# One pool of seven PSUM banks, with each stage taking the bank expected free first, in a fused attention and feed-forward kernel

## The reference

```python
x  = hidden_states                      # (8, 512, 128), fp32
x  = x + layernorm(attn(layernorm(x)))  # 16 heads: A = tril(taylor_exp(q) @ taylor_exp(k).T), y = A @ v, RMS norm, @ Wo
x  = x + layernorm(ffn(layernorm(x)))

def ffn(x):                             # six layers
    for i in range(6):
        x = attn_layer(shift_tokens(x), ...) + x   # local attention, window 32, 16 heads of 64
        x = ffn_layer(shift_tokens(x), ...) + x    # layernorm, W1, a * gelu(gate), W2
    return x

def attn_layer(x, Wqkv, qs, ks, Wo):
    q, k, v = split(x @ Wqkv)
    q, k = rotary(l2norm(q) * qs), rotary(l2norm(k) * ks)
    return local_attention(q, k, v) @ Wo           # softmax of 32 queries over their own and the previous 32 keys
```

## Time and profile before

| | |
|---|---|
| median of 3 runs | 3474.63 us (3473.0 to 3476.83) |
| the profiled execution | 3475.88 us, span of its profile 3474.1 us |
| busy: TensorE, VectorE, ScalarE, GpSimd | 92%, 80%, 73%, 59% |
| granted TensorE clock, mean | 0.979 |
| 700 to 3400 us: TensorE busy | 2506.3 of 2700 us |
| 700 to 3400 us: VectorE busy | 2296.6 us |
| 40 to 560 us: TensorE busy | 495.8 of 520 us |

### The profile page before, as it was taken

The page is one execution under the profiler, slowest core; times in us unless marked ns, Lnnn a source line. Parts: engine busy times, 40 slices in busy tenths (PEclk is TensorE's granted clock), DMA queues, the critical chain, the costliest instruction groups (busy, mean ns, idle before and its releaser), DMA issues.

```text
span 3474.1 us, 125058 instructions
## 1 busy us (share of the span) xinstructions
PE 3179.2 (92%) x52744; PEld 1975.5 (57%) x52744; DVE 2763.6 (80%) x3420; ACT 2536.5 (73%) x5866; POOL 2044.8 (59%) x1559
## 2 busy tenths in 40 slices
PE   7999997899999999999999899999999999999986
PEld 3444434566666566656666566666666665655553
DVE  3656657888888888888888888888888888888883
ACT  4666664778777777768787878787777777787784
POOL 0000006767677666767677777677767676766661
PEclk9999998999999999999999999999999999999998
DMA  3223324444444444444444444444444444434431
GB/s 110 77 75 80 80 57 135 140 142 136 145 149 145 135 134 145 144 140 137 140 136 148 138 151 138 140 141 152 146 142 137 134 146 139 143 127 145 137 130 31
DMA packets 271821, 447.01 MB, mean 129 GB/s; under 512 B 84254, under 2 KB 122396, under 8 KB 271132
## 3 DMA queue, kind: packets, MB, share of 16 engines
q1 hardware_dynamic: 244944, 422.50, 37.3%
q10 hardware_dynamic: 26316, 16.52, 1.7%
HBM read 124.21 MB, written 7.34 MB: 38 GB/s over the span
## 4 chain that ended last, share of the span: by engine, by line
PE 47%; DVE 24%; ACT 13%; issue 7%; SPq 3%; DMA 2%; POOL 2%; DVEq 0%; ACTq 0%; POOLq 0%
PE PS L542 47%; DVE TPB L938 8%; ACT SC L1245 8%; DVE SM L973 2%; DVE MX L962 2%; ACT SX L1221 2%; DMA RB<-root_scratch 2%; DVE NV L953 2%; DVE NV L951 1%; DVE PP L981 1%; POOL K L1332 1%; DVE H L1006 1%; SPq L477 1%; DVE NV L955 1%; ACT H L1024 1%
## 5 line engine op out<-in xcount | busy, mean ns | idle before, releaser
L938 DVE SCALAR_TENSOR_TENSOR TPB<-PS,VEC,C 128x1024 f32<-128x1024 f32 x768 | 959.1, 1269 | 98.7 <-ACT SX L1221 91.2
L1245 ACT ACTIVATE SC<-PS,BQ,RQ 128x64 f32<-128x64 f32 x3072 | 977.7, 437 | 40.0 <-DVE BQ L967 39.8
L1221 ACT ACTIVATE SX<-PS 128x512 f32<-128x512 f32 x768 | 468.6, 638 | 355.0 <-PE PS L542 347.9
L1332 POOL TENSOR_TENSOR K<-K,RB 128x512 f32<-128x512 f32 x384 | 496.2, 1292 | 286.8 <-DMA RB<-root_scratch 273.4
L1358 POOL TENSOR_TENSOR SC<-SC,RC 128x1024 f32<-128x1024 f32 x192 | 366.1, 1907 | 409.3 <-DVE RC L975 409.3
L542 PE MATMUL PS<-LXH,LH 128*128 128x512 f32 x768 | 379.2, 494 | 153.3 <-DVE TPB L938 145.9
L1350 POOL TENSOR_TENSOR K<-TPB,TR 128x512 f32<-128x512 f32 x384 | 499.2, 1300 | 0.0
L1350 POOL TENSOR_TENSOR Q<-TPB,TR 128x512 f32<-128x512 f32 x384 | 497.6, 1296 | 0.0
L542 PEld LDWEIGHTS PS<-PP,VV 64*64 64x64 f32 x12288 | 279.8, 136 | 149.7 <-issue 146.2
L542 PE MATMUL PS<-PP,VV 64*64 64x96 f32 (+1 forms) x12288 | 352.6, 250 | 4.3 <-DMA PP<-PX 2.0
L542 PE MATMUL PS<-AOT,LO 128*128 128x512 f32 x768 | 342.4, 599 | 0.0
(11 more groups left out here) (166 smaller groups left out, 5862.8 us busy)
## 6 DMA issues: line engine op xcount, KB each, us to landing
TR<-TPB SPq DMA_DIRECT2D x768, 256.0 KB, 2.7
RB<-root_scratch SPq DMA_DIRECT2D x768, 128.0 KB, 3.0
PP<-PX SPq DMA_DIRECT2D x576, 64.0 KB
PP<-PP SPq DMA_DIRECT2D x384, 64.0 KB, 2.4
WS<-in_wqkv ACTq DMA_DIRECT2D x72, 128.0 KB, 2.5
PP<-PX SPq DMA_DIRECT2D x192, 48.0 KB
QA<-TH SPq DMA_DIRECT2D x128, 64.0 KB, 2.1
QA<-TL SPq DMA_DIRECT2D x128, 64.0 KB, 2.1
```

Of the source, the lines that this page charges most:

```text
L938: e.scalar_tensor_tensor(TPB[:, n % 3:4 + n % 2:3 + n % 2 - n % 3, w, :], g, VEC[:, l, 9 + w:10 + w], C[:, at:at + 1024].rearrange("p (o c ...
L1221: e.activation(SX[i % 3][:, :], bk("PJ", key)[:, :], ACT.Square).then_inc(sem["pj_act"], 1)
L1245: p = e.activation(SC[m % 2][:, g, :, :].rearrange("p x k -> p (x k)"), bank[s][:, at:at + 64], ACT.Exp, bias=BQ[m % 2][:, g:g + 1], scale ...
L1332: e.tensor_tensor(dst, dst, RB[n % 2][:, :], ALU.mult).then_inc(sem["pr_pool"], 1)
```

## The change

All seven banks but bank 4 form one ring. Each claim says until when the planner expects the bank to be held (`held`, the difference of two places), and `take` gives the bank whose `until` is smallest. S1 and PV claim two banks each with `pair`, and each reads its banks through `bk`. Since the two banks need not be neighbours, MX becomes two reductions and PVn two copies. SX gets a fourth buffer. `PLACE` isn't changed.

```diff
-        self.ring, self.busy = [], {}
+        self.ring, self.busy, self.until, self.now = [], {}, {}, 0
...
-                at = self.ring.pop(0)
-                self.ring.append(at)
+                at = self.take(self.ring, 1, self.now)[0]
...
+    def take(self, ring, n, until):
+        banks = sorted(ring, key=lambda at: self.until.get(at, 0))[0:n]
+        for at in banks:
+            ring.remove(at)
+            ring.append(at)
+            self.until[at] = until
+        return banks
...
         for t, i, f, a, kw in sorted(plan, key=lambda e: e[:2]):
+            o.now = t
             f(*a, **kw)
...
+        if kind == "end":
+            o.until[o.bank["N2", (kind, b), 0]] += SLOT * (P["EN"][2] - P["EN"][1])
...
     def switch():
-        o.first = [o.busy[i] for i in early]
-        o.ring = [5, 6, 7]
+        o.ring = [0, 5, 6, 7] + early
+        o.busy[0] = ("as_act", 24 * NB)
         o.busy[5] = ("ao_act", NB)
...
-    def group(st, i, by, value):
-        ring = early or o.ring
-        at = ring.pop(0)
-        ring.append(at)
+    def group(st, i, by, value, held=0):
+        at = o.take(early or o.ring, 1, o.now + SLOT * max(held, 0))[0]
...
+    def pair(st, key, by, value, held):
+        for i, at in enumerate(o.take(o.ring, 2, o.now + SLOT * max(held, 0))):
+            o.hold(at, st, key, i)
+            o.busy[at] = (by, value)
+        o.put(st, *key)
...
-            lay(z + j + P["VP"], group, "VP", 8 * u + j, "vp_act", 8 * u + j + 1)
+            lay(z + j + P["VP"], group, "VP", 8 * u + j, "vp_act", 8 * u + j + 1, P["VC"] - P["VP"])
...
-            lay(n + P["PJ"][w], group, "PJ", i, "pj_dve", i + 1)
+            lay(n + P["PJ"][w], group, "PJ", i, "pj_dve", i + 1, P["PT"][w] - P["PJ"][w])
...
+            lay(n + P["S1"], pair, "S1", (m,), "s3_act", 4 * m + 4, max(P["S3"]) - P["S1"])
...
+            lay(n + P["PV"][0], pair, "PV", (m, 0), "pv_act", m + 1, P["PVn"] - P["PV"][0])
...
-        SX = [sb(f"SX{i}", [128, L]) for i in range(3)]
+        SX = [sb(f"SX{i}", [128, L]) for i in range(4)]
...
-                    if m:
-                        on.wait_ge("s3_act", 4 * m)
+                    for s in range(2):
+                        free(on, st, key, s)
...
-                        if p:
-                            on.wait_ge("pv_act", p)
+                        for x in range(2):
+                            free(on, st, key, x)
...
-                    e.tensor_reduce(MX[:, :], g, AX_X, ALU.max).then_inc(sem["s1_dve"], 1)
+                    for s in range(2):
+                        g = bk("S1", key, s).rearrange("p (g k) -> p g k", k=64)
+                        p = e.tensor_reduce(MX[:, 8 * s:8 * s + 8], g, AX_X, ALU.max)
+                    p.then_inc(sem["s1_dve"], 1)
...
-                    if i > 2:
-                        on.wait_ge("ss_pe", i - 2)
+                    if i > 3:
+                        on.wait_ge("ss_pe", i - 3)
...
-                    e.copy(AOT[:, 2 * p % 8:2 * p % 8 + 2, :], PS[:, 2:4, :]).then_inc(sem["pv_act"], 1)
+                    for x in range(2):
+                        y = e.copy(AOT[:, 2 * p % 8 + x, :], bk("PV", (p, 0), x))
+                    y.then_inc(sem["pv_act"], 1)
```

More of the change, by code:

```diff
@@ L256, in order @@
         for j in range(8):
-            lay(z + j + P["VP"], group, "VP", 8 * u + j, "vp_act", 8 * u + j + 1)
+            lay(z + j + P["VP"], group, "VP", 8 * u + j, "vp_act", 8 * u + j + 1, P["VC"] - P["VP"])
             lay(z + j + P["VC"], o.put, "VC", 8 * u + j)
-        lay(z + P["WO"][0], group, "WO", u, "wo_dve", 2 * u + 2)
+        lay(z + P["WO"][0], group, "WO", u, "wo_dve", 2 * u + 2, P["WO"][3] - P["WO"][0])
         for i in range(1, 4):
@@ L262, in order @@
         lay(z + P["F1"], group, "F1", u, "f1_act", 2 * u + 2)
-        lay(z + P["F2"], group, "F2", u, "f2_dve", 3 * u + 1)
+        lay(z + P["F2"], group, "F2", u, "f2_dve", 3 * u + 1, P["F2n"] - P["F2"])
         lay(z + P["F2n"], o.put, "F2n", u)
@@ L290, in order @@
             m = n // 2
-            for st in ("S1", "MX", "SU", "NP", "TT", "PX", "PY", "PVn"):
+            lay(n + P["S1"], pair, "S1", (m,), "s3_act", 4 * m + 4, max(P["S3"]) - P["S1"])
+            for st in ("MX", "SU", "NP", "TT", "PX", "PY", "PVn"):
                 lay(n + P[st], o.put, st, m)
@@ L294, in order @@
                 lay(n + P["S3"][i], o.put, "S3", m, i)
-            for i in range(2):
-                lay(n + P["PV"][i], o.put, "PV", m, i)
+            lay(n + P["PV"][0], pair, "PV", (m, 0), "pv_act", m + 1, P["PVn"] - P["PV"][0])
+            lay(n + P["PV"][1], o.put, "PV", m, 1)
     for b in range(NB):
@@ L691, in tensor_program @@
                     for c in range(4):
-                        p = mm(nb[32 * c:32 * c + 32, 0:128], sel, SX[i % 3][:, 128 * c:128 * c + 128], i % 8 == 0, i % 8 == 7,
+                        p = mm(nb[32 * c:32 * c + 32, 0:128], sel, SX[i % 4][:, 128 * c:128 * c + 128], i % 8 == 0, i % 8 == 7,
                                skip_group_check=True)
@@ L705, in tensor_program @@
                     m, = key
-                    for name, value in [] if m else o.first:
-                        on.wait_ge(name, value)
-                    if m:
-                        on.wait_ge("s3_act", 4 * m)
+                    for s in range(2):
+                        free(on, st, key, s)
                     for r in range(4):
@@ L713, in tensor_program @@
                             at = 64 * s + 32 * (r > 0)
-                            mm(bank[s][32 * r:32 * r + 32, :], identb[k, at:at + 32], maskb[k, :], True, False, skip_group_check=True)
+                            mm(bk(st, key, s)[32 * r:32 * r + 32, :], identb[k, at:at + 32], maskb[k, :], True, False, skip_group_check=True)
                     on.wait_ge("pr_pool", 2 * m + 2)
@@ L722, in tensor_program @@
                                 for s in range(2):
-                                    p = mm(bank[s][32 * r:32 * r + 32, at + first:at + 64],
+                                    p = mm(bk(st, key, s)[32 * r:32 * r + 32, at + first:at + 64],
                                            Q[64 * s:64 * s + 64, hp, 32 * j:32 * j + 32],
@@ L750, in tensor_program @@
                                 at = 128 * c + 64 * t
-                                y = mm(bank[2 + x][64 * s:64 * s + 64, at:at + 32 * n], VV[k, c, 64 * h:64 * h + 64],
+                                y = mm(bk(st, (p, 0), x)[64 * s:64 * s + 64, at:at + 32 * n], VV[k, c, 64 * h:64 * h + 64],
                                        PP[p % 2][k, 0:n, 8 * s + 4 * x + c, :], rho == 0 and c == 0, rho == 1 and c == 3,
@@ L957, in vector_program @@
                     m, = key
-                    g = PS[:, 0:2, :].rearrange("p s (g k) -> p (s g) k", k=64)
                     on.wait_ge("s1_pe", m + 1)
@@ L1217, in scalar_program @@
                     i, = key
-                    if i > 2:
-                        on.wait_ge("ss_pe", i - 2)
+                    if i > 3:
+                        on.wait_ge("ss_pe", i - 3)
                     on.wait_ge("pj_pe", i + 1)
-                    e.activation(SX[i % 3][:, :], bk("PJ", key)[:, :], ACT.Square).then_inc(sem["pj_act"], 1)
+                    e.activation(SX[i % 4][:, :], bk("PJ", key)[:, :], ACT.Square).then_inc(sem["pj_act"], 1)
                 elif st == "NM1":
@@ L1244, in scalar_program @@
                         at = 64 * (g - 8 * s)
-                        p = e.activation(SC[m % 2][:, g, :, :].rearrange("p x k -> p (x k)"), bank[s][:, at:at + 64], ACT.Exp,
+                        p = e.activation(SC[m % 2][:, g, :, :].rearrange("p x k -> p (x k)"), bk("S1", (m,), s)[:, at:at + 64], ACT.Exp,
                                          bias=BQ[m % 2][:, g:g + 1], scale=r[:, g:g + 1])
```

## The result

The changed kernel takes 3489.95 us (median of 5 runs, 3488.88 to 3499.14), the kernel before 3474.63 (median of 5, 3466.29 to 3482.14): a ratio of 1.0053, 95% interval 1.003 to 1.0076. The medians differ by 15.3 us; the ratio stands for 18, and its interval for 10 to 26. It was forecast at 3494 with 3481 to 3511. The two profiled executions, 3489.13 and 3475.88 us, differ by 13.3 us.

A forecast was written before the change was run, and what follows sets the result against it. TensorE, busy 92% of the span, was taken to bound the kernel, so only its idle time could be won. Terms 0 + 10 + 8 + 1.5 = +19.5 us gave 3494 us on the median, range 3481 to 3511.

The forecast's parts named there:

- The bank rule: Feed-forward projections: 568 of 707 keep their reader, PJ 2 and PJ 14 included; gain 0 to 2 us, taken 0.
- Rival (a): Bank waits at PJ 2 and PJ 14 go, up to 146 us; half won, 3400 us; chance 0.05.
- The start: Claims before time 0 all take bank 6, so early products wait for evacuations; 6 to 11 us, taken 8.
- the one for the lower level: At the start, TensorE staying at the lower clock through the broken stretch: six stages x 0.72 = 4.3 us more.
- PV 0: First PV of a unit waits for PT 7's bank, late in 27 of 46 units; 0 to 14 us, taken 10.
- Rival (b): PJ 14's wait swallows PV 0's delay, early slack most of the start: no difference, 3478 us; chance 0.09.
- The splits: MX 0.09 us longer on VectorE, PVn 0.04 on ScalarE, mostly covered; MX 0 to 9 us, taken 1.5; PVn 0.
- Rival (c): Added 17 us on VectorE and 8 us on ScalarE count in full: clearly slower, 3521 us; chance 0.06.
- The long BQ: VectorE's BQ behind MX, 0.95 us, ends with a GpSimd instruction, so it shortens and absorbs MX's later end.
- Square buffer: Fourth buffer at PQ: the wait for a buffer never ends last, so 0 us.
- The sum: All terms over the whole kernel: 0 + 10 + 8 + 1.5 = +19.5 us, 3494 on the median; chance 0.80.
- the sum of evacuations: At the start, product-to-evacuation times of the one-bank stretch: 18.5 us with restarts, last AV 7.9 later, 6.4 left.

The follow-up runs named there:

- e6_meas: Changed kernel with the start mended and the planner's holding times replaced by a table set from the trace; ratio to the kernel before 1.0061.
- e7_half: As e6_meas, table set anew, first bank of a score pair counted free after ScalarE's first eight exponentials; ratio to the kernel before 1.0001.
- e2_onebank: Kernel before, with all bank claims at planned times below 0 taking bank 6; ratio to the kernel before 1.0022.
- e5_pvwait: Kernel before, with one added wait: PV 0 of each unit also waits for PT 7 of the unit; ratio to the kernel before 1.0032.
- e3_split: Kernel before, with only MX split into two reductions and PVn into two copies, banks as before; ratio to the kernel before 1.0005.
- e8_half3: As e7_half, holding times set again from that kernel's trace so that RQ 1 gets a free bank; ratio to the kernel before 1.0075.
- e1_start: Changed kernel, with a bank not yet taken counted free since long ago, so the start alternates two banks; ratio to the kernel before 1.0033.

## Why the prediction was right

**The bank rule** was right, and it decided the sign. The waits for L938 stayed near 146 us (152.9), one at PJ 2 and one at PJ 14. Rival (a) falls by the change itself. e6_meas goes further: it wasn't only the planner's guess of the holding times that kept the two waits alive. And e7_half shows that (a)'s price was too high as well: it took 73 of the 109 us before PJ 2 and PJ 14 away, and the time didn't fall. The prediction's count of 568 of 707 projections comes out as 578 of 717 from the two orders of work, which changes nothing.

**The start**: the mechanism was right, the size too small. I took 8 us from 6 to 11, and the first AS came 11.9 us later, outside that range. From the second AL to the last AV before AS 0 I had added up 18.5 us, and it took 22.5 (26.93 to 49.44). The term that was mis-sized is the one for the lower level, which I had put into the bounds (4.3 us) and mostly left out of the value. A further 0.9 us I hadn't counted at all: the second AL itself starts at 26.93 instead of 26.07. With the broken stretch the products kept their slow durations until 64 us, through AS and AY as well, where those of the kernel before were fast from 31 us, with a second stretch at the lower level from about 41 to 51 us (granted clock 0.57 in the 5 us from 40 and 0.50 in those from 45). In the total it is worth 8 us by e2_onebank, whose interval (2 to 13) holds 11.9 too; that this is the 8 I took is luck.

**PV 0**: I took 10 us. Its wait is 7.3 to 9.2 us in 41 units, and the isolated wait costs 11 us in the total (6 to 16). The profile names "issue" as its releaser, not PT as I had said. Rival (b), that PJ 14 swallows it, falls by e5_pvwait.

**The splits**: 0.07 us a pair instead of 0.09, and 1.5 us was taken; e3_split gives 0.05% with 0 inside its interval. Rival (c) falls with it. The long BQ was in the trace as read: between 700 and 3400 us 45 of 46 MX 0 have one of over 0.25 us behind them after the change, and the mean at MX 0 is 0.68 us instead of 0.77, so the later start was absorbed there. At MX 3 the mean isn't shorter: 0.54 after, 0.52 before.

**Square buffer**: no effect shows, as said.

**The sum** was 19.5, the median moved by 15.3. Sizes of the right order and some luck: the interval of the ratio alone reaches from 10 to 26 us.

Not settled: why the pooled kernels idle 6 to 9 us more before PJ 14 (e3_split has 2 of it, e5_pvwait none), why e6_meas runs at a lower clock, and what e6_meas and e8_half3 lose behind PJ 720.

## What to carry to other kernels

Before giving an in-order engine more buffers, list for each of its waits which instruction last read the buffer under the new rule: here 578 of the 717 projections behind 700 us kept the very same releaser. A buffer pool also couples stages that had nothing to do with each other, and one such wait a unit cost 11 us here. And a large wait in one place can be the visible end of a loop through several engines: taking 62 us away before PJ 2 brought nothing, since waits came back at RQ 1, inside S1 and at F4g. Last, put the granted clock of every run beside its time before explaining a difference: of e6_meas' 21 us it goes with 18.

## What the runs showed of the hardware

The clock at the start surprised me. TensorE rose from its lower to its higher level at 31 us after a solid stretch of products from 22.64 to 30.4 us; with that stretch broken by waits of 0.4 to 2.2 us the rise came at 64 us, and a 512-column product took 0.63 instead of 0.39 us until then. e2_onebank has the late rise too, e1_start the early one (the first 0.39 at 65.24 and at 32.05 us). What brings the rise isn't shown: ahead of 64 us the products had run without a gap from 49.44 us on, longer than in the first stretch. In both traces the granted clock is recorded only from the rise on, so the level ahead of it is read from durations: the AY products (PA,VA, 128x384 x4) take 1.55 us at 60.38 in the changed kernel, as they do at 47.66 in the kernel before, where the granted clock is 0.50, and 0.87 at 55.44. Of the 11.9 us some 5.5 are left for the clock and the later second AL if the waits have the 6.4 of the sum of evacuations; that split is an estimate and not measured.

The Trainium skill ("Trainium Kernel Development and Optimization", Best Practices) says that consistent bubbles can mean that PSUM ran out. In this case the bubbles were waits for PSUM banks, 146 us of them, and yet e7_half, with more than half of those at the projections gone, stands at 1.0001: here the rule found the shortage, not what it costs.
